# Graph layer with residual layer norm on one core: the last normalisation split between VectorE (odd row tiles) and ScalarE (even row tiles), and a new written order for the first 16 tiles

## The reference, cut to what matters

```python
mask = adj > 0
head = mask.astype(float32)
head = head / maximum(sqrt(sum(head * head, axis=-1, keepdims=True)), 1e-12)
inc = adj + head                       # 4096 x 4096
edge = (inc @ x) / sum(inc, axis=-1, keepdims=True)
y = x + edge
out = (y - mean(y)) / sqrt(var(y) + 1e-5)      # per row of 256
```

## Time and profile before

| what | value |
|---|---|
| median of three runs | 411.33 us (410.71 to 412.14) |
| profiled execution, its own time | 410.89 us |
| its span on the core | 409.1 us |
| PE busy | 389.3 us, 95% |
| ACT busy | 371.4 us, 91% |
| DVE busy | 364.2 us, 89% |
| POOL busy | 346.3 us, 85% |
| granted TensorE clock, whole span | 1.0 |

### The profile page before, as it was taken

One profiled execution on the slowest core, in us unless ns is written; L12 is line 12 of the kernel. 1 busy time (PEld: TensorE's weight loads), 2 busy tenths in 40 slices (PEclk: granted clock), 3 DMA queues, 4 the chain that ended last, 5 costly groups with the idle time before them and its releaser, 6 DMA issues.

```text
span 409.1 us, 8775 instructions
## 1 busy us (share of the span) xinstructions
PE 389.3 (95%) x2224; PEld 343.1 (84%) x2224; DVE 364.2 (89%) x757; ACT 371.4 (91%) x507; POOL 346.3 (85%) x222
## 2 busy tenths in 40 slices
PE   1689999999999999999999999999999999999995
PEld 0668889988888878888888888888888888888884
DVE  0897999999999999999999999999999999999932
ACT  4967999999999999999999999999999999998530
POOL 3111599999999999999999999999999999999970
PEclk9999999999999999999999999999999999999999
DMA  8999997576677667667666665767666666670020
GB/s 237 269 253 253 264 261 215 168 238 204 200 221 222 190 187 215 190 206 222 200 208 205 195 205 191 208 216 214 197 210 201 196 206 192 215 218 27 27 64 13
DMA packets 36183, 80.00 MB, mean 196 GB/s; under 512 B 9536, under 2 KB 17728, under 8 KB 36160
## 3 DMA queue, kind: packets, MB, share of 16 engines
q1 hardware_dynamic: 35776, 78.68, 66.1%
q10 hardware_dynamic: 384, 1.05, 0.8%
HBM read 75.50 MB, written 4.19 MB: 195 GB/s over the span
## 4 chain that ended last, share of the span: by engine, by line
PE 83%; POOL 4%; issue 4%; SPq 4%; DMA 3%; DVE 1%; ACT 1%; POOLq 0%; ACTq 0%
PE edge L1307 46%; PE edge L1321 23%; PE edge L1258 12%; POOL inc_split L564 3%; DMA x_stage<-in_x_dram 3%; SPq L156 3%; PE sums L1253 1%; SPq L179 1%; DVE incT L767 1%; POOL inc_split L578 0%; PE sums L1232 0%; SPq L184 0%; POOL small L548 0%; DVE inc L751 0%; ACT scaled L251 0%
## 5 line engine op out<-in xcount | busy, mean ns | idle before, releaser
L564 POOL TENSOR_TENSOR inc_split<-incT,inc_split 128x960 fp32r<-128x960 f32 x120 | 269.4, 2272 | 2.4 <-ACT inc_split L262 0.5
L1307 PE MATMUL edge<-x_split,inc_split 128*128 128x512 f32 (+1 forms) x930 | 223.4, 392 | 0.1
L1307 PEld LDWEIGHTS edge<-x_split,inc_split 128*128 128x128 f32 x930 | 168.1, 188 | 32.8 <-ACT inc_split L262 0.9
L751 DVE SCALAR_TENSOR_TENSOR inc<-raw,scaled 128x1024 f32<-128x1024 f32 x128 | 154.3, 1206 | 3.3 <-ACT scaled L251 2.4
L767 DVE STREAM_TRANSPOSE incT<-inc 128x1024 f32<-128x1024 f32 x128 | 156.3, 1230 | 0.7 <-PE edge L1258 0.4
L251 ACT ACTIVATE scaled<-raw,small 128x1024 f32<-128x1024 f32 x128 | 141.1, 1107 | 2.8 <-DVE inc L751 1.2
L240 ACT ACTIVATE sign_out<-raw 128x1024 int8<-128x1024 f32 x128 | 133.7, 1045 | 4.5 <-DMA raw<-in_adj_dram 4.3
L1321 PEld LDWEIGHTS edge<-x_split,inc_split 128*128 128x128 f32 x900 | 112.2, 191 | 2.3
L1321 PE MATMUL edge<-x_split,inc_split 128*128 128x256 f32 x900 | 113.5, 283 | 0.0
L262 ACT CAST inc_split<-incT 128x960 fp32r<-128x960 f32 x90 | 86.5, 984 | 0.7 <-DVE incT L767 0.7
L583 POOL TENSOR_TENSOR small<-small 128x1 f32<-128x1 f32 x24 | 13.2, 554 | 37.2 <-DVE small L733 37.0
(11 more groups left out here) (42 smaller groups left out, 138.8 us busy)
## 6 DMA issues: line engine op xcount, KB each, us to landing
raw<-in_adj_dram SPq DMA_DIRECT2D x504, 128.0 KB, 2.5
rows<-in_x_dram SPq DMA_DIRECT2D x32, 128.0 KB, 2.1
out_dram<-rows SPq DMA_DIRECT2D x32, 128.0 KB, 1.7
x_stage<-in_x_dram SPq DMA_DIRECT2D x12, 256.0 KB, 9.4
raw<-in_adj_dram ACTq DMA_DIRECT2D x8, 128.0 KB, 5.1
x_stage<-in_x_dram SPq DMA_DIRECT2D x4, 192.0 KB, 13.6
x_native<-in_x_dram SPq DMA_DIRECT2D x4, 64.0 KB, 5.7
```

What stands on the lines that cost most here:

```text
L564: nc.gpsimd.tensor_tensor(lo_of(s, q), incT[:, s, 0:SPLIT, q, :], hi_of(s, q).bitcast(fp32), ALU.subtract).then_inc(lo_by_pool, 1)
L751: nc.vector.scalar_tensor_tensor(inc[:, q, :], raw[:, s, q, :], 0.0, scaled[q % 2][:, :], ALU.is_gt, ALU.add, accum_out=part_sums[:, s, 0, ...
L1307: last = nc.tensor.matmul(edge[s][:, c0:c1], inc_split[s][:, 0, b, :, :].rearrange("p q j -> p (q j)"), x_split[:, b, :, :].rearrange("p h ...
```

## The change

1. The shift and ACT's normalisation are kept for even tiles only, now from tile 0 on (16 tiles, 0 to 30). Odd tiles 1 to 29 are normalised by DVE in one `tensor_scalar` of 128 x 256 in SBUF, `normalise_odd`, at the place where `shift_of` of the odd tile stood. `normalise_by_dve` goes.
2. The stores wait for one of two semaphores, by parity.
3. The written orders of the first tiles are new on DVE, ACT, POOL and PE, and reach to tile 15 now; the loop runs from u = 8. In the loop itself nothing else moves.

```diff
             def store(t, s):
-                sp.wait_ge(result_ready, t + 1)
+                sp.wait_ge(result_by_dve if s else result_by_act, t + 2 - s)
                 sp.dma_start(out_rows[t], y[:, s, :]).then_inc(stored[s], 16)
...
-            def normalise(t, s):
-                act.wait_ge(shift_ready, t - 3)
+            def normalise_even(t, s):
+                act.wait_ge(shift_ready, t + 2)
                 nc.scalar.activation(y[:, s, :], y[:, s, :], ACT.Identity, scale=norm_rstd[:, s, G:G + 1],
-                                     bias=shift[:, s:s + 1]).then_inc(result_ready, 1)
+                                     bias=shift[:, s:s + 1]).then_inc(result_by_act, 2)
...
-            with act.Fori(7, PAIRS - 2) as u:
+            with act.Fori(8, PAIRS - 2) as u:
...
                 scale_quarter(2 * u + 1, 1, 1)
-                normalise(2 * u - 3, 1)
                 round_quarter(2 * u, 0, 2)
...
-                normalise(2 * u - 2, 0)
+                normalise_even(2 * u - 2, 0)
                 round_quarter(2 * u + 1, 1, 2)
...
+            def normalise_odd(t, s, alone=0):
+
+                if alone:
+                    dve.wait_ge(rstd_ready, alone)
+                else:
+                    dve.wait_ge(norm_ready, t + 5 - EARLY)
+                nc.vector.tensor_scalar(y[:, s, :], y[:, s, :], mean_var[:, s, 0:1], norm_rstd[:, s, G:G + 1],
+                                        ALU.subtract, ALU.mult).then_inc(result_by_dve, 2)
+
...
-            with dve.Fori(7, PAIRS - 2) as u:
+            with dve.Fori(8, PAIRS - 2) as u:
...
                 transpose_quarter(2 * u, 0, 3)
-                shift_of(2 * u - 3, 1)
+                normalise_odd(2 * u - 3, 1)
                 inc_quarter(2 * u + 1, 1, 0)
```

More of the change, by code:

```diff
@@ L346, in _ @@
             scale_early(5, 1)
+            sign_early(6, 0)
             sign_early(6, 1)
@@ L680, in _ @@
             low_quarter(13, 1, 3)
-            with pool.Fori(7, PAIRS - 2) as u:
+            round_quarter(14, 0, 1)
+            norm_of(15, 1)
+            low_quarter(14, 0, 0)
+            low_quarter(14, 0, 1)
+            low_quarter(14, 0, 2)
+            low_quarter(14, 0, 3)
+            norm_of(16, 0)
+            round_quarter(15, 1, 1)
+            low_quarter(15, 1, 0)
+            low_quarter(15, 1, 1)
+            low_quarter(15, 1, 2)
+            low_quarter(15, 1, 3)
+            with pool.Fori(8, PAIRS - 2) as u:
                 norm_of(2 * u + 1, 1)
@@ L888, in _ @@
             count_early(2, 1)
+            inc_quarter(2, 0, 0)
             split_x_lo(2)
-            inc_quarter(2, 0, 0)
             split_x_lo(3)
@@ L895, in _ @@
             count_early(2, 3)
+            inverse_degree(0, 0)
             transpose_quarter(2, 0, 1, slot_split=False)
@@ L1053, in _ @@
             degree(9, 1)
-            inc_quarter(11, 1, 1)
             transpose_quarter(11, 1, 1)
@@ L1074, in _ @@
             inverse_degree(10, 0)
+            inc_quarter(12, 0, 3)
             count_of(13, 1)
@@ L1101, in _ @@
             variance_eps(11, 1)
-            with dve.Fori(7, PAIRS - 2) as u:
+            inc_quarter(14, 0, 0)
+            degree(12, 0)
+            inc_quarter(14, 0, 1)
+            inverse_degree(12, 0)
+            transpose_quarter(14, 0, 0)
+            y_first(12, 0, 6)
+            inc_quarter(14, 0, 2)
+            transpose_quarter(14, 0, 1)
+            y_second(12, 0)
+            count_of(15, 1)
+            inc_quarter(14, 0, 3)
+            statistics(12, 0)
+            transpose_quarter(14, 0, 2)
+            transpose_quarter(14, 0, 3)
+            mean_variance(12, 0)
+            normalise_odd(11, 1)
+            inc_quarter(15, 1, 0)
+            variance_eps(12, 0)
+            degree(13, 1)
+            inc_quarter(15, 1, 1)
+            inverse_degree(13, 1)
+            transpose_quarter(15, 1, 0)
+            y_first(13, 1, 6)
+            inc_quarter(15, 1, 2)
+            y_second(13, 1)
+            transpose_quarter(15, 1, 1)
+            count_of(16, 0)
+            statistics(13, 1)
+            inc_quarter(15, 1, 3)
+            shift_of(12, 0)
+            mean_variance(13, 1)
+            transpose_quarter(15, 1, 2)
+            transpose_quarter(15, 1, 3)
+            variance_eps(13, 1)
+            with dve.Fori(8, PAIRS - 2) as u:
                 inc_quarter(2 * u, 0, 0)
@@ L1382, in _ @@
+            tile(13, 1, {("hi", 16): lambda: sum_quadrants(13, 1)})
+            tile(14, 0, {("hi", 18): lambda: sum_quadrants(14, 0)})
+            tile(15, 1, {("hi", 11): lambda: sum_quadrants(15, 1)})
             SUMS_AT = ("hi", 12)
-            with pe.Fori(7, PAIRS - 1) as u:
+            with pe.Fori(8, PAIRS - 1) as u:
                 for s in range(2):
```

339 lines of the change are left out of this document (171 added, 168 removed).

## The result

The changed kernel takes 421.3 us (419.24 to 421.78, 4 runs), the kernel before beside it 411.02 (410.28 to 412.14, 4 runs): ratio 1.0223, interval 1.0181 to 1.0264. It is slower, as forecast, but by more than my range allowed (up to 419.2). The profiled execution took 421.43 us with a span of 419.6, 10.5 us more than that of the kernel before.

A forecast was written before the change was run, and what follows sets the result against it. PE was taken to bound the kernel: 410.89 us profiled − 0.5 for the first 16 tiles + 5.05 for loop and tail = 415.4, with part of the 0.44 to the median 415.5 us; range 409.5 to 419.2.

The forecast's parts named there:

- PE bounds the kernel, a tile is 11.55 us, and no order gains more than 1.95 us.: Whole kernel: PE busy 389.3 of 409.1 us, standing still only 1.95 us in the first 16 tiles once it runs.
- The odd normalisation waits for POOL; its place sets its price, 1.97 us.: Loop: DVE arrives 0.35 us behind the start of POOL's 2.23 us low part and gets through 1.97 us late.
- First time late costs 0.45, later ones 0.95 by a circle of 24.05 us.: Loop: PE stops 0.45 us at first, then 0.95 per iteration, as two tiles take 24.05 where PE needs 23.1.
- The gap in front of the high part of odd tiles: Sign in the loop's profile: PE gaps ahead of odd tiles' high part, released by ACT's rounding; pairs take about 24 us.
- One of six gets in ahead of POOL.: Loop, tiles 15 to 25: one normalisation passes at no cost, the next costs 0.45 again; loop and tail sum 5.05 us.
- First 16 tiles, -0.5 us.: Start: the new orders gain 0.5 us, with bounds of −1.95 and +3.8 us.
- One warm-up matmul fewer ... is hidden by that load.: PE's start: one warm-up matmul fewer before 28.2 us costs nothing, since the first load of `x` lasts until then.
- Stores: "nothing is added": Odd tiles' stores and the residual loads behind them come about 1.3 us later; `y_first` is 1.9 late anyway, so no cost.
- B: Rival, faster: DVE's instruction is through within 1.4 us, PE never stops in the loop; 409.4 us, chance 0.16.
- C: Rival, nothing: the loop absorbs the block, the first tiles keep their stalls or swap them; 411 us, chance 0.09.
- A: Rival: DVE's block in the loop is absorbed every other time; 412.4 us, chance 0.19.
- D: Rival: blocks from tile 5 on cost PE 0.95 each, plus a full loop; 418.5 us middle, 421 most, chance 0.08.

The follow-up runs named there:

- one_port: The changed kernel with DVE's odd normalisation also writing an accumulator (accum_out): 412.85 us, ratio 1.0020.
- two_columns: The changed kernel with DVE normalising only 2 of the 256 columns of an odd tile: 420.96 us, ratio 1.0225.
- one_earlier: The changed kernel with DVE's odd normalisation ahead of the even tile's last transpose in loop and tail: 414.05 us, ratio 1.0044.
- sum_later: The changed kernel with PE's small sum of even tiles three chunks later in the loop: 421.55 us, ratio 1.0228.
- combined: The changed kernel with ACT's tile 2 normalisation two scalings earlier, odd normalisation before the last transpose in loop and tail, tile 15's small sum at chunk 14: 413.89 us.
- norm2_first: The changed kernel with ACT's normalisation of tile 2 two scalings earlier: 420.42 us, ratio 1.0203.
- warm_combined: combined with the sum of tile 1's third quarter ahead of tile 0's first chunk and 12 warm-up matmuls behind it: 411.75 us, ratio 0.9986.
- one_later: The changed kernel with DVE's odd normalisation behind the odd tile's first inc_quarter in loop and tail: 417.37 us, ratio 1.0129.
- orders_only: The changed kernel's first 16 tiles, but odd tiles from 13 on normalised by ACT as in the kernel before: 414.04 us, ratio 1.0037.
- warm_act: Like warm_combined, but ACT normalises the odd tiles from 13 on, as in the kernel before: 413.90 us, ratio 1.0039.
- placed: warm_combined with DVE's normalisation of tile 3 moved ahead of y_second of tile 4, and tile 5's ahead of the last transpose: 411.50 us, ratio 0.9970.
- placed_act: warm_act with DVE's normalisations of tiles 3 and 5 moved earlier as in placed: 411.54 us, ratio 0.9970.

## Why the prediction was wrong in size, step by step

The sum had -0.5 us for the first 16 tiles and 5.05 for the loop and the tail, 4.55 in all. The profiles show 2.70 up to tile 15 and 7.80 behind it, 10.50 in all. Both terms failed, and by about as much: 3.2 and 2.75 us.

**PE bounds the kernel, a tile is 11.55 us, and no order gains more than 1.95 us.** No run speaks against it. The best kernels of the study are 0.9 us under the kernel before by the medians, 1.2 by the ratio.

**The odd normalisation waits for POOL; its place sets its price, 1.97 us.** This held to a tenth: 2.06 us at 340.15, behind a low part that began at 339.80 (339.80 + 2.27 + 0.1 to 0.2). one_port, two_columns and one_earlier each show it from another side.

**First time late costs 0.45, later ones 0.95 by a circle of 24.05 us.** The size was nearly right (24.17), the way was not. I let the circle run count, POOL, DVE's exit, DVE to the next count, with DVE no longer waiting for PE. The runs show it closed through ACT: exit, even shift, ACT's normalisation, roundings and signs, PE's odd small sum, count. sum_later fits this ring and not the one through PE's even sum. I took the slack of 0.8 us behind ACT's roundings as the place where PE would stop, and did not follow ACT on to the signs behind them. The gap in front of the high part of odd tiles, released by ACT's rounding, that I had named as a sign is not there: the waits from 219 to 388 us name none.

**One of six gets in ahead of POOL.** This failed, and it is one of the two mis-sized terms. I had the margin at 0.15 us (16.2 - 16.0, so rather 0.2) from a DVE that doesn't wait for PE. It does wait, and its count behind that wait is the one that starts POOL, so the margin is 5.15 - 4.80 = 0.35 us every time. Only tile 13's, in the first iteration with its phase not yet set, got in. Tiles 15 to 27 were all blocked, and the stretch from tile 15 to 31 lost 7.07 us with 0.73 more in the tail, where the sum had 5.05 for both. Some 0.6 of the 7.07 are tile 15's own and not the block's: that tile takes 12.16 us, takes 12.18 in one_port too, where nothing is blocked, and 11.53 in combined with its small sum at chunk 14.

**First 16 tiles, -0.5 us.** This failed in sign. They lost 2.7 us by tile 15 and 3.3 by tile 16 (222.73 against 219.42). Three causes were seen. Tile 2's normalisation on ACT comes late, and with it store, residual and `adj` loads (norm2_first: 1.35 us in tile 7). Odd normalisations stand at places that are now and then blocked: where tile 3's is caught, tile 6 takes 12.71 and 12.72 us (one_earlier, warm_combined), else 11.54 to 11.87; in the changed kernel it got in. And PE is idle at 19 to 23 us. PE's gaps I had called hidden by the load at 28.2 us: "One warm-up matmul fewer ... is hidden by that load." It is hidden only while the clock stays up. In the changed kernel's profile it was 0.51 between 24 and 27 us and tile 1 started 0.94 late; in seven of the ten profiled kernels with that start it fell, and tile 1 started at 31.8 to 33.3 us instead of 30.7 to 31.1. What took tile 14 its 1.1 us (12.84 against 11.72 before) stays open, as its order is the same in kernels that don't lose there.

**Stores: "nothing is added".** True in the loop of the changed kernel, where the waits above name no load. It was not safe: norm2_first and one_later show that this chain begins to cost as soon as a normalisation moves 2 us in the first tiles or 1 us in the loop.

**The rivals.** B and C fell with the 2 us block. A fell because the normalisation never got in every other time. D, "the first tiles pay too" (418.5 in the middle, 421 at most), is what happened at its upper end, though mostly by other mechanisms than its own: of the blocks in front of tile 13 only that at 126.35 us (2.17) was long. I gave it 0.08; that three unread risks in a rewritten start (order of stores, phase of the blocks, PE's gaps) would all be harmless deserved less trust.

## What to carry to other kernels

A DVE `tensor_scalar` in SBUF beside a busy GpSimd cost the rest of GpSimd's running instruction here, whether it had 256 columns (1.98 us) or 2 (1.94): put it in front of or inside a short GpSimd instruction, not just behind the start of a long one, and one swapped line can be worth 7 us. When such a wait closes a ring, look for the event from which both partners are counted: if it is the same, the collision repeats every time. When the written order of a start changes, check three things before calling it free: which loads stand behind a store that now comes later, what the idle gaps do to PE's clock, and whether an instruction comes within a tenth of a us of a boundary that decides 0.4 or 2.5 us.

## What the runs showed of the hardware that I had not expected

- A DVE `tensor_scalar` of 128 x 2 waited 1.94 us beside POOL; the form that writes an accumulator took 504 ns at the same places and never waited. DVE's shift of 128 x 1 (L890), between the same POOL instructions, took 0.17 us.
- DVE's normalisation of tile 3 came within 0.15 us of POOL's boundary: 0.40 us long in some profiles and 2.52 in others of kernels with the same order there (101.64 in sum_later, 101.76 in one_earlier).
- The granted clock fell to 0.50 in some kernels with the same start and not in others (norm2_first kept 1.00 with 1.77 busy us from 20 to 23; the changed kernel had 0.81 there). In norm2_first, one_earlier and sum_later, the three that kept it, PE's 12 warm-up matmuls before 20 us took 2.91 us, not 1.58 as in the changed kernel; the first wait was then gone and the second 1.3 us, not 2.08. In orders_only they took 2.91 us as well, the second wait was 1.51, and the clock was 0.70 from 23 to 27.

What stays open: why the same warm-up matmuls take 1.58 or 2.91 us, why warm_act lost what warm_combined did not, why `adj` comes late now and then (tile 14 of the changed kernel, tile 12 of placed), what stops PE for 0.8 us in tile 8 of placed, and why placed_act's runs spread over 3.4 us.
